# Token tiles of four query positions of all images behind the attention, up projections of two experts by token block, filler matmuls among the relative values

## The reference

```
p   = 64 patches of 16 x 16 pixels of every image                    (32, 64, 256)
h   = (mish(p W1' + b1') * (p W2' + b2')) W3' + b3 + positions       (32, 64, 128), noisy W1', W2'
h   = [class token; h]                                               (32, 65, 128)
q, k, v = layernorm(h) Wq + bq, ... ; 8 heads of 16
a   = softmax((q k' + q . rel_k[clip(k - q)]) / sqrt(128))
o   = a v + sum_k a . rel_v[clip(k - q)]
h   = h + (o Wo + bo)
x   = layernorm(h);  r = softmax(x Wr' + br);  the two largest of 8 experts keep their r, the others get 0
h   = h + sum_e r_e (gelu(x W1_e + b1_e) W2_e + b2_e)               experts: 128 -> 256 -> 128
```

## Time and profile before

| | |
|---|---|
| median of 3 runs | 276.25 us (274.6 to 277.44) |
| the profiled execution | 276.12 us, span of its records 274.3 us, mean granted clock 0.985 |
| busy, share of the span | PE 89%, DVE 60%, ACT 47%, POOL 22% |
| chain that ended last | PE 61%, DVE 24%, ACT 4%, DMA 4%, issue 3%, POOL 2% |
| attention loop | about 70 to 115 us |
| relative values | about 122 to 136 us |
| projection, second layernorm, router | about 137 to 157 us |
| bias products, experts | about 167 to 270 us |

### The profile page before, as it was taken

One profiled execution on the slowest core, in us unless ns is written; L12 is line 12 of the kernel. 1 busy time (PEld: TensorE's weight loads), 2 busy tenths in 40 slices (PEclk: granted clock), 3 DMA queues, 4 the chain that ended last, 5 costly groups with the idle time before them and its releaser, 6 DMA issues.

```text
span 274.3 us, 6405 instructions
## 1 busy us (share of the span) xinstructions
PE 243.3 (89%) x2519; PEld 209.3 (76%) x2519; DVE 163.9 (60%) x512; ACT 129.6 (47%) x432; POOL 60.5 (22%) x77
## 2 busy tenths in 40 slices
PE   0799997999886888895799978999999999999993
PEld 0665564899674656675689966999999999999993
DVE  0476888635679999999689463333333324242453
ACT  1543057942487999960015794052526262626100
POOL 8930122292023443563027000000000000000000
PEclk9999999999999999999999996899999999999998
DMA  6960000000000000270000000000000000000015
GB/s 218 279 142 2 1 0 0 2 4 2 0 0 4 2 2 2 88 223 5 5 2 0 4 0 0 2 0 0 2 0 0 2 1 2 0 4 0 0 25 133
DMA packets 6554, 7.95 MB, mean 29 GB/s; under 512 B 833, under 2 KB 5295, under 8 KB 6396
## 3 DMA queue, kind: packets, MB, share of 16 engines
q1 hardware_dynamic: 5260, 6.32, 8.2%
q10 hardware_dynamic: 720, 0.87, 1.2%
q0 software_dynamic: 544, 0.35, 0.5%
HBM read 6.47 MB, written 1.06 MB: 27 GB/s over the span
## 4 chain that ended last, share of the span: by engine, by line
PE 61%; DVE 24%; ACT 4%; DMA 4%; issue 3%; POOL 2%; ACTq 0%; DVEq 0%
PE banks L987 56%; DMA region_d<-in_L_tok_W_sw 4%; DVE stb L720 3%; DVE top L736 3%; DVE stb L640 2%; ACT region_d L510 2%; DVE stats L625 2%; DVE xnT L833 2%; PE banks L1186 2%; DVE region_c L761 2%; POOL rstd L309 2%; DVE mv L628 1%; DVE h L616 1%; DVE ntop L743 1%; DVE tmpx L828 1%
## 5 line engine op out<-in xcount | busy, mean ns | idle before, releaser
L977 DVE SCALAR_TENSOR_TENSOR KT<-banks,vbd,KT 128x128 f32<-128x128 f32 (+1 forms) x136 | 38.0, 344 | 61.1 <-PE banks L987 61.1
L510 ACT ACTIVATE region_d<-banks,vecs 128x416 f32<-128x416 f32 x80 | 45.6, 611 | 55.2 <-PE banks L987 55.2
L987 PE MATMUL banks<-w_all,region_d 128*128 128x128 f32 (+1 forms) x544 | 64.1, 278 | 0.0
L987 PEld LDWEIGHTS banks<-w_all,region_d 128*128 128x128 f32 (+1 forms) x544 | 62.2, 190 | 1.6 <-issue 0.6
L488 ACT ACTIVATE region_e<-banks,ntop 128x64 f32<-128x64 f32 x128 | 38.2, 326 | 7.0 <-DVE rsum L754 3.5
L987 PE MATMUL banks<-x_hi,w_hi 128*128 128x416 f32 x80 | 29.9, 373 | 0.9 <-ACT region_d L510 0.9
L987 PE MATMUL banks<-x_lo,w_hi 128*128 128x416 f32 x80 | 28.6, 358 | 0.0
L987 PE MATMUL banks<-x_hi,w_lo 128*128 128x416 f32 x80 | 28.6, 357 | 0.0
L488 ACT ACTIVATION_READ_ACCUMULATOR region_e<-banks,ntop 128x1 f32 x128 | 27.9, 218 | 0.0
L343 POOL TENSOR_TENSOR region_e<-region_e,rsum 128x512 f32<-128x512 f32 (+1 forms) x16 | 16.5, 1032 | 37.3 <-DVE rsum L754 37.3
L987 PEld LDWEIGHTS banks<-x_hi,w_hi 128*128 128x128 f32 x80 | 15.3, 191 | 2.8 <-issue 1.4
(11 more groups left out here) (219 smaller groups left out, 381.5 us busy)
## 6 DMA issues: line engine op xcount, KB each, us to landing
region_a<-in_x SPq DMA_DIRECT2D x2, 512.0 KB, 6.2
region_a<-in_x SPq DMA_DIRECT2D x1, 1024.0 KB, 11.0
w_sb<-in_L_ffn_W SPq DMA_DIRECT2D x1, 1024.0 KB, 5.6
out<-KT SPq DMA_DIRECT2D x8, 128.0 KB, 2.4
region_d<-in_L_attn_rel_v SPq DMA_DIRECT2D x2, 260.0 KB, 9.8
kc<-in_consts ACTq DMA_DIRECT2D x1, 336.0 KB, 5.7
region_d<-in_L_tok_eps_in ACTq DMA_DIRECT2D x2, 128.0 KB, 7.5
region_d<-in_L_tok_W_w ACTq DMA_DIRECT2D x1, 128.0 KB, 7.9
```

The lines of the kernel that those rows point to most:

```text
L510: a.activation(HB[:, e % 2, s, blk * FB:(blk + 1) * FB], bank[h_bank(i)][:, 0:FB], ACT.Gelu, bias=vecs[:, v:v + 1]).then_inc(S["gelu_ok"], 1)
L977: last = v.scalar_tensor_tensor(acc[0:m, t, :], bank[out_bank(u)][0:m, i * C:(i + 1) * C], comb[0:m, t, e:e + 1], acc[0:m, t, :], op0=ALU. ...
L987: return t_.matmul(o, l, r, start=start, stop=stop)
```

## The change

- **Order of tokens.** Behind the attention `OT` is held by position first (`OTq`): a tile is four query positions of all 32 images. A group of 16 positions is then exactly a block of 512 tokens, and block n can be projected when group n of the relative values is added. The residual stream `h0` is in order of images; SP writes it to the output tensor in memory when pair 5's scores are added, and reads it back in the new order when pair 10's are.
- **Output.** The result's tiles have four positions on four bands of 32 partitions: four transfers a group, where there were two.
- **Class key.** POOL takes the difference and repeats the class probabilities in the loop, two pairs at a time; PE turns them in the loop; DVE multiplies 256 columns in odd iterations ahead of `add`, and the product and the value bias are added as DVE copies the outputs.
- **Class products** go to four column groups of 32, in the first two iterations.
- **Relative values** come in half groups between which the projections stand; one identity product (`keep_warm`) stands behind every four positions of the first one and a half groups. Group 3 is in bank 0.
- **Second layernorm.** DVE takes all four sums, ACT normalises (scale and bias, the bias is -mean times the reciprocal root, by POOL), DVE takes all low parts.
- **Up products** of experts 0 and 1 alternate by token block, and so do their gelus.

```diff
-OP_BANKS = (5, 6, 2, 3)
+OP_BANKS = (1, 2, 3, 5)
+REL_BANKS = (4, 5, 6, 0)
+        UNITS = [(e, blk, s) for blk in range(5) for e in range(2) for s in range(2)]
+        UNITS += [(e, blk, s) for e in range(2, E) for blk in range(5) for s in range(2)]
...
 @block.sync
+            oq = out[:, 1:QC, :].rearrange("b (t f) c -> f b t c", f=4)
+            sp_.wait_ge(S["h0o_ok"], 1)
+            sp_.wait_ge(S["st_ok"], 5)
+            for b2 in range(2):
+                sp_.dma_start(ov[b2, 1:QC, :, :], h0v[64 * b2:64 * b2 + 64, :, :]).then_inc(S["d_h0s"], 16)
+            sp_.wait_ge(S["d_h0s"], 32)
+            sp_.wait_ge(S["st_ok"], 10)
+            for f in range(4):
+                sp_.dma_start(h0v[32 * f:32 * f + 32, :, :], oq[f]).then_inc(S["d_h0q"], 16)
...
-                    for b2 in range(2):
-                        sp_.dma_start(ov[b2, 1:QC, 4 * g:4 * g + 4, :],
-                                      acc[64 * b2:64 * b2 + 64, 4 * g:4 * g + 4, :]).then_inc(S["d_out"], 16)
+                    for f in range(4):
+                        sp_.dma_start(oq[f][:, 4 * g:4 * g + 4, :],
+                                      acc[32 * f:32 * f + 32, 4 * g:4 * g + 4, :]).then_inc(S["d_out"], 16)
...
 @block.gpsimd
+            def difference(p):
+                pool.wait_ge(S["top_ok"], p + 1)
...
+                g.tensor_tensor(SP[p % 4][:, 512:520], ntop[:, o], nSc[:, p * H:(p + 1) * H], ALU.subtract)
+            def repeat(u):
+                pool.wait_ge(S["pc_ok"], 2 * u + 2)
...
+            for p in range(PAIRS + 2):
+                if p < PAIRS:
+                    difference(p)
+                if p >= 2:
+                    normalised(p - 2)
+                    if p % 2 == 1:
+                        repeat((p - 3) // 2)
...
 @block.scalar
+            def norm2(n):
+                act.wait_ge(S["nmr_ok"], n + 1)
...
+                    last = a.activation(ST[n % 2][0:m, i * C:(i + 1) * C], KT[0:m, t * C:(t + 1) * C], ACT.Identity,
+                                        bias=nmr[0:m, t:t + 1], scale=rstd[0:m, t:t + 1])
+            norm2(0); evac_x2(0); norm2(1); gelu 0, 1; evac_x2(1); norm2(2); gelu 2, 3; evac_x2(2); norm2(3); norm2(4)
+            gelu 4, 5; evac_x2(3); gelu 6, 7; evac_x2(4); gelu 8, 9; then the router's exponential
...
 @block.vector
-                    v.tensor_tensor(SP[p % 4][:, 512:520], ntop[:, o], nSc[:, p * H:(p + 1) * H], ALU.subtract)
+                if u is not None:
+                    if new is not None:
+                        dve.wait_ge(S["s1_ps"], new + 1)
+                    class_key(u)
                 if new is not None:
                     add(new)
...
-                v.tensor_copy(OT[:, 256 * u:256 * u + 256].rearrange("p (b q) -> p b q", b=4), o[:, :, 0:NPATCH])
+                v.scalar_tensor_tensor(OTq[:, :, 4 * u:4 * u + 4].rearrange("p q b -> p b q"), o[:, :, 0:NPATCH],
+                                       vecs[:, V_BV:V_BV + 1], own(u), op0=ALU.add, op1=ALU.add)
...
+            attended(0); attended(1); residual(0); attended(2); residual(1); low(0); attended(3); attended_class()
+            residual(2); low(1); residual(3); class rows; residual(4); low(2); low(3); low(4)
...
 @block.tensor
+            for g in range(4):
+                r = 4 * g + i
+                mm(bank[7][32 * g:32 * g + 32, 0:P], q0w[:, 24 - H * i:56 - H * i], KT[:, r * P:(r + 1) * P], ...)
...
+            def filled(n, part):
+                for i in range(part[0], part[-1] + 1, 4):
+                    relative(n, range(i, i + 4))
+                    keep_warm(1, spare=3)
+            filled(0, range(16)); filled(1, early); project(0); relative(1, late); relative(2, early); project(1)
+            relative(2, late); relative(3, early); project(2); turn2(0); relative(3, late); relative_class()
+            keep_warm(2); project(3); the class rows' projection
+            up(0, 0); turn2(1); router(0); up(1, 0); up(0, 1); turn2(2); router(1); up(1, 1); up(0, 2); turn2(3)
+            router(2); up(1, 2); turn2(4); up(0, 3); router(3); router(4); up(1, 3); up(0, 4)
```

More of the change, by code:

```diff
@@ L335, in _, with normalised @@
             ins.then_inc(S["h0o_ok"], 1)
-            for p in range(PAIRS):
+            g.memset(lg[:, PAIRS * E:NT * E], 0.0).then_inc(S["lz_ok"], 1)
+            g.tensor_tensor(clsr[0:IMG, :], clsr[0:IMG, :], bob[0:IMG, :], ALU.add).then_inc(S["cb_ok"], 1)
+            def difference(p):
+                o = slice(8 * (p % 2), 8 * (p % 2) + 8)
+                pool.wait_ge(S["top_ok"], p + 1)
+                if p >= 4:
+                    pool.wait_ge(S["pc_ok"], p - 3)
+                g.tensor_tensor(SP[p % 4][:, 512:520], ntop[:, o], nSc[:, p * H:(p + 1) * H], ALU.subtract)\
+                    .then_inc(S["dc_ok"], 1)
+            def normalised(p):
                 pool.wait_ge(S["r_ok"], p + 1)
@@ L364, in _ @@
             deviation2(2)
-            low(0)
             deviation2(3)
-            low(1)
             deviation2(4)
@@ L523, in _ @@
             a.preload_act_table_set("gelu_and_others")
-            for i in range(8, 18):
+            for i in range(10, 18):
                 gelu(i)
@@ L901, in residual, with low @@
                     moments(KT, n, 1, IMG, "ve2_ok")
-            def norm2(n):
-                full = n < NBLK
-                normalise(KT, n, TPB if full else 1, P if full else IMG, "rstd2_ok", "xn2_ok", "x2T_ps", n - 1)
-            residual(0)
-            dve.wait_ge(S["opc_ps"], 1)
-            v.tensor_tensor(KT[0:IMG, TOK:TOK + C], bank[4][0:IMG, 128:256], clsr[0:IMG, :], ALU.add)\
-                .then_inc(S["h1c_ok"], 1)
-            for n in range(1, 5):
-                residual(n)
-                norm2(n - 1)
-            norm2(4)
-            for n in (2, 3, 4):
+            def low(n):
                 b = slice(n * BLK, n * BLK + (BLK if n < NBLK else IMG))
@@ L919, in _ @@
                 dve.wait_ge(S["x2T_ok"], n + 1)
-                v.tensor_tensor(x_lo[:, b], xn2T[:, b], x_hi[:, b].bitcast(F32), ALU.subtract).then_inc(S["xloD_ok"], 1)
+                v.tensor_tensor(x_lo[:, b], xn2T[:, b], x_hi[:, b].bitcast(F32),
+                                ALU.subtract).then_inc(S["xlo_ok"], 1)
+            attended(0)
+            attended(1)
+            residual(0)
+            attended(2)
+            residual(1)
+            low(0)
+            attended(3)
+            attended_class()
+            residual(2)
+            low(1)
+            residual(3)
+            dve.wait_ge(S["opc_ps"], 1)
+            v.tensor_tensor(KT[0:IMG, TOK:TOK + C], bank[6][0:IMG, 0:C], clsr[0:IMG, :], ALU.add)\
+                .then_inc(S["h1c_ok"], 1)
+            residual(4)
+            low(2)
+            v.memset(combP, 0.0).then_inc(S["cz_ok"], 1)
+            low(3)
+            low(4)
             lv = lg[:, :].rearrange("p (t e) -> p t e", e=E)
@@ L1170, in scores @@
                     pe.wait_ge(S["st_ok"], p)
+                if p >= 6 and p % 2 == 0:
+                    turn_pc((p - 6) // 2)
                 for b2 in range(2):
@@ L1278, in _, with relative_class @@
-            last.then_inc(S["w2_ps"], 1)
-            def residual(n):
-                mm(bank[OP_BANKS[n]][:, :], ident, h0[:, n * BLK:(n + 1) * BLK], True, False)
+                if 15 in part:
+                    last.then_inc(S["w2_ps"], 1)
+            def relative_class():
+                mm(bank[4][:, IMG:2 * IMG], kc[:, K_E8T:K_E8T + P], p0x[:, :])
+                for j in range(PJ):
+                    last = mm(bank[4][32 * j:32 * j + 32, 0:IMG], RVBD[:, 32 * NPATCH:32 * NPATCH + 32],
+                              PT[:, j, :, NPATCH])
+                last.then_inc(S["w2_ps"], 1)
```

311 lines of the change are left out of this document (165 added, 146 removed).

## The result

The changed kernel takes **279.1 us** (median of 17 runs, 276.92 to 281.11). The kernel before took 276.34 in the same sessions (17 runs, 274.31 to 278.17): ratio 1.0085, interval 1.0059 to 1.0112. So it is 0.6 to 1.1% slower: a difference clear of noise, though 1.0085 lies within the 1% that I had called no change (the median itself is 0.1 above that band's 279.0). It is 2.1 us above the 277.0 that I had forecast, and above the forecast's own range (275.7 to 278.5); only the wide range (272.8 to 280.2) holds it. The profiled execution took 279.76 us for a span of 277.9; 1.86 lie around the span, as before.

What follows compares the result with a forecast made beforehand. TensorE's unbroken expert work (173.7 to 269.6) was taken as the bound, so its start and the tail count. Terms: -2.8 (start) +0.1 (clock) +3.6 (issues) = +0.9, 277.0 us; own range 275.7 to 278.5, wide range 272.8 to 280.2.

Steps and rivals of the forecast that it cites:

- Start of the long stretch: TensorE's unbroken expert work: its bias products start at 163.8 instead of 166.61, -2.8 us.
- Clock behind the bias products: PE's half clock after the bias products costs the same as before plus 0.1 us, bounds -3.4 and +3.4.
- Output: Stores at the kernel's end: sixteen SP issues of 0.64 us put the class rows' issue at 275.5, not 271.9: +3.6 us.
- Loop: Attention loop on DVE: odd iterations 2.94 us, even 2.34; last pair's maximum at 112.1, not 113.86.
- Start of the relative values: After the attention, PE's first relative value starts at 119.3 instead of 122.5.
- Pauses among them: PE's relative values: 256 instructions per 3.46 us including pauses; the second block of outputs ready at 127.3.
- Blocks up to the first up product: DVE, POOL, ACT and PE passing token blocks on: PE's first up product at 138, not 148.21.
- From there to the router: PE, ACT and DVE holding each other up after the first up product: last router product at 153.8 to 154.3, before 155.9.
- the router comes no earlier: Rival: ACT's queue from norm2(2) to evacuation 4 delays the router past 155.9, no gain left, 279.8 us; chance 0.22.
- Router to bias products: Router end to bias products: ACT's table load at 155.0, 2.9 earlier; later steps at present distances, bias products at 163.8.
- Rival 1: Store issues at the end are cheap, about 0.4 us each: tail costs 0.4, kernel 273.8 us; chance 0.17.
- The residual stream's trip through memory: Residual stream written and read back behind pairs 5 and 10, some 30 us before first use: hidden.

Runs made afterwards that it cites:

- experiment 11: gelus_first_filled without the six identity products between the relative values of positions 0 to 23: 269.81 us.
- Experiment 9: The changed kernel in its own ACT queue order, with identity products in all the PE gaps: 273.36 us.
- gelus_first_filled: The changed kernel with gelus 4 and 5 ahead of blocks 3 and 4's normalisation on ACT, and identity products in the four gaps left on PE: 271.08 us.
- one_expert_first_filled: The changed kernel with expert 1's up products behind the last router product instead of alternating, and identity products in four places on PE: 270.87 us.
- two_store_queues: one_expert_first_filled with the output transfers of bands 2 and 3 issued by ACT instead of SP: 269.23 us.

## Why the prediction came out as it did

The wide range and the side were right, the working was not: of its three terms one held, and the errors of the other two have opposite signs. So it is luck that the time fell where it did. Start of the long stretch: -2.8 predicted, +3.0 measured. Clock behind the bias products: +0.1 predicted, 0 measured. Output: +3.6 predicted, +0.6 measured. The errors are +5.8, -0.1 and -3.0, together the 2.7 between +0.9 and +3.6 in the span (by the medians +2.8).

**Loop: right in time, by a little luck.** The last maximum was to come at 112.1 and came at 112.35. Even iterations take 2.33 (predicted 2.34). Odd ones take 3.11, not 2.94: the new product costs 0.32, close to the 0.35 that I took, but the output copy with two operands holds DVE for 0.50 where the plain one took 0.33. I had priced the new instruction and not the one that was exchanged. A pair of iterations so takes 5.44 us, more than the 5.33 of before. The first five gave the 1.5 that I had reckoned with (13.85 us from the first to the sixth maximum, before 15.30), and the ten behind them lost 0.5 instead of gaining 0.3. Counted from its first maximum the loop is only 0.9 shorter, not 1.8; 0.6 more came from an earlier start, which is within the spread of 71.4 to 73.2.

**Start of the relative values: right**, 119.65 against 119.3. **Pauses among them: wrong.** I had carried over the pace of 256 instructions in 3.46 us. In the changed kernel there are no pauses, since fillers and projections stand between; the second outputs were ready at 127.9, not 127.3, because the fillers take 0.42 each outside of any pause. Two errors that cancel again; experiment 11 takes them apart. The rule that I cited (the Trainium skill, Runtime: NRT & Kernel Launch, "Instruction fetch mechanics", by which fetch hides behind the pace of issue) is closer to this kernel than my pace was, but 0.90 us of pause without the fillers shows that it doesn't hold for dense blocks, if the pauses are fetch. No run isolates that, but the packets of the instruction queue in the traces fit it: in before and in no_fillers_among_values all five pauses of PE end 1.3 to 1.5 us after a packet of 16 KB has landed (122.5, 125.95 and 133.0 before). Such packets come in the changed kernel too (landed at 121.25 and 124.97), without a pause.

**Blocks up to the first up product: right.** 138.55 against 138; the fourth block's variance is written at 144.41 against 144.1.

**From there to the router: this step failed.** I wrote "norm2(3) 145.8, gelus 147.1, up 147.8, ... routers 153.8 to 154.3". Measured: norm2(3) begins at 146.28, the gelus end at 149.3, up(0,2) runs from 148.95 to 151.0, and the routers end at 160.4. That is 6.1 us, of two kinds.
- *ACT's queue, 2.2 to 2.3.* One normalisation piece costs 0.39 us (five from 146.28 to the gelu at 148.22), four 1.65 to the end of the last, where I had taken 1.1, and the fifth, of block 4, stands in the same row. POOL's two operations take until 146.25 behind a variance of 144.41, 1.8 where I had reckoned with 1.3. I had both bounds (0.8 to 2.4) and took the low side. My chain didn't add up either: 144.1 and 1.3 and 1.1 are 146.5, not the 145.8 that I wrote, so 0.7 of the 2.2 is a slip. The Trainium skill has this price (ScalarE: Activation LUTs, "What ACT_TABLE_LOAD costs"): 280 ns and 0.833 per column with one pointer operand, 93 more for the second, 93 less back to back, so 0.39 a piece as an estimate for 128 columns. The trace agrees with its 0.39.
- *The clock, 3.8 to 4.1.* I looked for half clock only behind the bias products, where the kernel before has it. But I had myself written that PE's third up product waits for ACT, and PE had nothing to do from 146.3 to 148.95. The clock was at 1.2 GHz from 149.3 to about 176.6. Experiment 9 shows the size. The Trainium skill (TensorE: Matmul & The Clock Gate, "HAM oscillation — how this bites in real kernels") warns that idle gaps between bursts put PE back at the lower clock, and that the work behind them starts there. The trace agrees on the fall; but the first product behind the gap (148.95, 0.43 us) still ran at the full clock.

The rival that was worth 0.22, "the router comes no earlier", named the place (ACT's queue from norm2(2) to evacuation 4) and the point from which it decides (a router end past 156): this is what happened. Its price was wrong, since it had the full output term and no clock; the 279.8 that it gave is close to the 279.1 for the wrong reason.

**Router to bias products: right in sum.** Predicted 9.5 us, measured 9.2. ACT's table load came at 157.66, while the router was still running: it doesn't wait for the logits, only for the gelus ahead of it in the queue.

```profile
157.66 1.28 ACT L587 ACT_TABLE_LOAD   x1
161.60 0.32 ACT L587 ACTIVATE lg<-lg 128x136 f32<-128x136 f32 x1 [2.67 <-DVE lg L993]
```

I had let it start at 155.0, behind the logits. In gelus_first_filled, at full clock, the same stretch takes 8.8: 0.7 less than I had reckoned.

**Clock behind the bias products: right.** 7.4 us at 0.53, before 7.1 at 0.52. Filling it gives 3.0 to 3.2 in both kernels, close to the 3.4 of the prediction.

**Output: mis-sized by 3.0.** From start to start 16 x 0.64 became 16 x 0.48. Four issues then take 1.93 us, little more than DVE's pace of 1.79 a group, so they add 1.0 and not 3.6; and the class rows' transfer lands 0.5 sooner behind its issue, which I hadn't reckoned with. Rival 1 (issues at 0.4) was right in this part. The price that I had cited from the Trainium skill, about 50 ns on another path, isn't what SP shows either.

**The residual stream's trip through memory: right.** Issued at 80.4 and 95.4, landing after 5.4 and 4.6 us (medians), first used at 128.50.

## What to carry to other kernels

When work is moved ahead on one engine, look at what the engine that feeds it has queued there, and order that queue by who waits: here two gelus ahead of two normalisations were worth 2.1 us at equal clock. Price a new idle gap of PE by its own length and by all the work behind it at half clock; identity products in the gaps were worth 1.7 us in the kernel before and about 5 in the changed one. But filler products that stand in front of real ones, with no gap to fill, are paid for in full (0.42 us each here).

## What I had not expected of the hardware

- The same transfer's issue on SP takes 618 ns or 443 ns, by the transfers issued ahead of it: 64 partitions (596 to 701 ns) or 32 (342 to 457). The first of the sixteen is the shortest, 342; the first of the eight is the longest, 701.
- The clock is sensitive to small differences. In one_expert_first_filled the profiled run fell to a granted clock of 0.5 in a slice, and the same order and fillers in two_store_queues held 1.00. Kernels that keep the clock may also scatter less: 270.75 to 271.6 in five runs of gelus_first_filled against 276.92 to 281.11 in 17 of the changed one. The other filled kernels don't all show it (270.19 to 273.69 in five of one_expert_first_filled).
- Pauses of PE without a visible wait depend on what stands between small products: 0.74 to 1.58 us after blocks of 25 to 153 records before (the first two in the earlier trace rows), none in the changed kernel, 0.90 and 0.24 without the fillers.
